# A pair's second projection in the eight-tile form, and the LayerNorm steps laid out anew, in a two-layer graph attention kernel

## What is computed

```python
# 4 heads of 64; the 2048 columns of the scores fall into 8 segments of 256
q, k, v = x @ Wq.T + bq, x @ Wk.T + bk, x @ Wv.T + bv
scores = einsum(q, k) / sqrt(64)           # per head and segment
scores = clip(scores, -10, 10); scores = where(adj == 0, -10, scores)
ctx = sum over the segments of softmax(scores in the segment) @ v
out = layernorm(ctx @ Wo.T + bo + x) * gamma + beta     # "first LayerNorm"
x1 = layernorm(x + out)                                  # "second LayerNorm"
```

## Time and profile before

| | us |
|---|---|
| three runs | 4062.63 to 4076.89, median 4069.85 |
| the profiled execution's own time | 4073.17 |
| its span, first to last instruction | 4071.4 |
| mean granted clock of TensorE | 0.972 of full speed |
| busy: TensorE, VectorE, ScalarE, GpSimd | 3657.9, 3294.2, 2519.2, 2045.2 |

### The profile page before, as it was taken

One profiled execution on the slowest core, in us unless ns is written; L12 is line 12 of the kernel. 1 busy time (PEld: TensorE's weight loads), 2 busy tenths in 40 slices (PEclk: granted clock), 3 DMA queues, 4 the chain that ended last, 5 costly groups with the idle time before them and its releaser, 6 DMA issues. The chain is left out here.

```text
span 4071.4 us, 131728 instructions
## 1 busy us (share of the span) xinstructions
PE 3657.9 (90%) x55412; PEld 2507.9 (62%) x55412; DVE 3294.2 (81%) x3989; ACT 2519.2 (62%) x3554; POOL 2045.2 (50%) x1068
## 2 busy tenths in 40 slices
PE   5999999999999999999999999952998999899988
PEld 2656656655665665666565566421777777777777
DVE  6786787787688678678778768858889889899897
ACT  3665665566566566566566566631776776676777
POOL 1776776777677677677667767742011011011010
PEclk9999999999999999999999999976999999999999
DMA  5000010001000000001000100024110110101101
GB/s 211 3 34 13 13 45 13 13 14 44 13 14 34 13 24 34 13 13 45 13 13 14 44 13 13 13 68 175 32 52 21 53 51 23 53 27 46 32 21 42
DMA packets 106678, 145.05 MB, mean 36 GB/s; under 512 B 3792, under 2 KB 87632, under 8 KB 104016
## 3 DMA queue, kind: packets, MB, share of 16 engines
q1 hardware_dynamic: 104816, 135.80, 10.0%
q10 hardware_dynamic: 1248, 0.40, 0.1%
HBM read 102.63 MB, written 33.55 MB: 33 GB/s over the span
## 5 line engine op out<-in xcount | busy, mean ns | idle before, releaser
L373 ACT ACTIVATE probs<-probs 128x1024 f32<-128x1024 f32 x1024 | 1083.9, 1059 | 997.2 <-DVE probs L778 971.5
L269 POOL TENSOR_TENSOR psums<-probs 128x1024 f32<-128x1024 f32 x512 | 1265.6, 2473 | 788.4 <-ACT probs L373 757.1
L778 DVE SCALAR_TENSOR_TENSOR probs<-sc_ps,clip_hi 128x1024 f32<-128x1024 f32 x1024 | 1228.5, 1216 | 442.9 <-PE sc_ps L472 436.5
L485 PE MATMUL ctx_ps<-probs,v_rows 64*32 64x512 f32 x16256 | 1385.1, 593 | 0.0
L472 PE MATMUL sc_ps<-q_cols,k_cols 64*32 64x512 f32 x16384 | 1209.2, 593 | 96.9 <-DVE probs L778 88.5
L1242 PE MATMUL out_ps<-wh,e 128*128 128x257 f32 x4096 | 963.1, 388 | 168.4 <-DVE e L1384 162.3
L1242 PEld LDWEIGHTS out_ps<-wh,e 128*128 128x128 f32 x4096 | 777.1, 193 | 329.7 <-DVE e L1384 125.6
L485 PEld LDWEIGHTS ctx_ps<-probs,v_rows 64*32 64x32 f32 x16256 | 659.2, 107 | 250.2 <-issue 143.8
L472 PEld LDWEIGHTS sc_ps<-q_cols,k_cols 64*32 64x32 f32 x16384 | 548.1, 107 | 413.4 <-issue 293.6
L479 PE MATMUL den_ps<-psums,ones 64*32 64x512 f32 x4064 | 610.5, 599 | 54.2 <-ACTq L324 18.9
L1071 POOL TENSOR_TENSOR rstd<-var_eps,minus_half 128x4 f32<-128x4 f32 x32 | 68.4, 2138 | 1071.1 <-DVE var_eps L1344 1071.1
(11 more groups left out here) (97 smaller groups left out, 3325.6 us busy)
## 6 DMA issues: line engine op xcount, KB each, us to landing
x_cols<-in_xT SPq DMA_DIRECT2D x8, 2048.0 KB, 10.4
probs<-in_adjT SPq DMA_DIRECT2D x16, 1024.0 KB, 8.3
x_rows<-in_x SPq DMA_DIRECT2D x32, 512.0 KB, 4.9
x<-res SPq DMA_DIRECT2D x32, 512.0 KB, 3.3
x_in<-x SPq DMA_DIRECT2D x8, 2048.0 KB, 10.3
x_res<-x SPq DMA_DIRECT2D x32, 512.0 KB, 4.6
out<-h SPq DMA_DIRECT2D x32, 512.0 KB, 3.2
e<-in_adjT SPq DMA_DIRECT2D x8, 1024.0 KB, 7.8
```

Source lines behind the costliest of these rows:

```text
L269: pool.tensor_tensor(psums[:, q % 2, pair, :], probs[:, (SJ * q) % RING, pair, :], probs[:, (SJ * q + 1) % RING, pair, :], ALU.add).then_i ...
L373: act.activation(probs[:, n % RING, pair, :], probs[:, n % RING, pair, :], ACT.Exp, scale=DH ** -0.5).then_inc(s_exp, 1)
L485: return pe.matmul(ctx_ps[quad(h), z, :], v_rows[head_rows(r), n % JB, at:at + QUAD], probs[head_rows(r), n % RING, h, :], start=start, st ...
L778: dve.scalar_tensor_tensor(out=probs[:, n % RING, pair, :], in0=sc_ps[:, p, :, :], scalar=-LIM, in1=clip_hi[:, j, c * CW:(c + 1) * CW][:, ...
```

## The change

A pair with two projections gets its own order, `pair_with_two`: the second projection in the eight tiles too, its lower half beside the context part between the third and fourth scores, its upper half behind the fourth scores together with the rest of the contexts. ScalarE copies a second projection ahead of the exponential (n+1,1), not behind it. The projections are spread anew over the steps: seconds stand at the steps 1, 3, 9, 57, 59, 61 and 63 (before: 1, 5, 11, 53, 57, 59, 61), seven as before, and pairs 9 and 10 gain a first while pairs 13 and 14 lose theirs. VectorE's LayerNorm steps go to other slots: of `times_gamma`, `add_x`, `add_bo` and `add_beta` no pair has more than two, where pair k = 7 had three. `inverse_deviation` and `norm` follow by one pair, and the SyncE queue takes the load of x_cols, the load of x rows and the store of x1 in another order.

```diff
@@ -57,17 +57,18 @@
-    uses = {0: ("k", 3, 0), 1: ("v", 2), 2: ("k", 3, 1), 4: ("v", 3), 5: ("q", 1, 0), 10: ("v", 4), 11: ("q", 1, 1),
-            12: ("v", 5), 14: ("v", 6), 16: ("v", 7), 26: ("q", 2, 0), 28: ("q", 2, 1), 32: ("q", 3, 0),
+    uses = {0: ("v", 2), 1: ("k", 3, 0), 2: ("k", 3, 1), 3: ("q", 1, 0), 4: ("v", 3), 9: ("q", 1, 1), 10: ("v", 4),
+            12: ("v", 5), 14: ("v", 6), 16: ("v", 7), 18: ("q", 2, 0), 20: ("q", 2, 1), 32: ("q", 3, 0),
             34: ("q", 3, 1)}
...
-    NEXT = {48: ("q", 0, 0), 50: ("q", 0, 1), 52: ("k", 0, 0), 53: ("k", 0, 1), 57: ("k", 1, 0), 58: ("k", 1, 1),
-            59: ("v", 0), 60: ("k", 2, 0), 61: ("v", 1), 62: ("k", 2, 1)}
+    NEXT = {48: ("q", 0, 0), 50: ("q", 0, 1), 52: ("k", 0, 0), 57: ("k", 0, 1), 58: ("k", 1, 0), 59: ("v", 0),
+            60: ("k", 1, 1), 61: ("v", 1), 62: ("k", 2, 0), 63: ("k", 2, 1)}
     assert not set(uses) & set(NEXT)
...
     PRJ = len(order)
+    SECOND = [n for n in order if n % 2]
     FIRST = len(NEXT)
@@ -87,6 +88,10 @@
         return count(b, PRJ, FIRST + order.index(n) - skipped)
+
+    def second_number(b, n, more):
+        skipped = 0 if more else sum(other < n for other in NEXT if other % 2)
+        return count(b, len(SECOND), SECOND.index(n) - skipped)
@@ -170,6 +175,8 @@
         s_waited = sem("waits_over")
+        s_stored = sem("stores_begun")
+        s_part2 = sem("first_rows_of_second_projection_added")
         s_pool = sem("segment_summed")
@@ -218,17 +225,18 @@
                 sp.wait_ge(s_n[1], count(b, NC * T, (c + 1) * T))
+                sp.sem_inc(s_stored, 1)
                 sp.dma_start(batch_of(x1, b)[c * CW:(c + 1) * CW, :].rearrange("(t p) f -> p t f", p=P),
...
             def chunk(b, c, prev, more):
-                if prev == 2:
-                    store_x1(*back(b, c - 2, NC))
-                load_rows(b, c)
                 if c == 2 and more:
...
                                  .rearrange("(k p) n -> p k n", p=P)).then_inc(s_xT, 16)
+                load_rows(b, c)
+                if prev == 2:
+                    store_x1(*back(b, c - 2, NC))
@@ -291,7 +299,7 @@
                         inverse_deviation(*back(b, c - 1, NC), 0)
-                    if k == 2 and prev == 2:
+                    if k == 3 and prev == 2:
                         inverse_deviation(*back(b, c - 2, NC), 1)
@@ -380,22 +388,22 @@
                     if prev and k in (6, 7):
-                        norm(*back(b, c - 1, NC), 1 + 2 * (k - 6), 0)
-                    if prev == 2 and k in (3, 4):
-                        norm(*back(b, c - 2, NC), 2 * (k - 3), 1)
+                        norm(*back(b, c - 1, NC), 2 * (k - 6), 0)
+                    if prev == 2 and k in (4, 5):
+                        norm(*back(b, c - 2, NC), 2 * (k - 4), 1)
                     exponential(b, n, 1)
...
                     exponential(b, n + 1, 0)
-                    if prev and k in (5, 6):
-                        norm(*back(b, c - 1, NC), 2 * (k - 5), 0)
-                    if prev == 2 and k in (3, 4):
-                        norm(*back(b, c - 2, NC), 2 * (k - 3) + 1, 1)
-                    exponential(b, n + 1, 1)
+                    if prev and k in (6, 7):
+                        norm(*back(b, c - 1, NC), 2 * (k - 6) + 1, 0)
+                    if prev == 2 and k in (4, 5):
+                        norm(*back(b, c - 2, NC), 2 * (k - 4) + 1, 1)
                     if second:
                         take(*second, use_number(b, n + 1, more))
+                    exponential(b, n + 1, 1)
@@ -604,6 +612,72 @@
+            def pair_with_two(b, n, at, q, of, use, number, of2, use2, number2, nth):
+                scores(b, n, 0)
+                sums_ready(at, q)
+                pe.wait_ge(s_prjfree, number + 1)
+                waited()
+                for h in range(HEADS):
+                    den_part(q, 0, h)
+                    prj_part(of, use, 1, 0, h, 0, start=True)
+                for h in range(HEADS):
+                    prj_part(of, use, 1, 0, h, 1)
+                contexts_ready(at, q)
+                for h in range(HEADS):
+                    ctx_part(q, 0, 0, 0, h, start=True)
+                    prj_part(of, use, 1, 1, h, 0)
+                for h in range(HEADS):
+                    last = prj_part(of, use, 1, 1, h, 1)
+                last.then_inc(s_part, 1)
+                scores(b, n, 1)
+                other_rows_done(at, q, 0)
+                for h in range(HEADS):
+                    prj_part(of, use, 0, 0, h, 0)
+                    last = den_part(q, 1, h)
+                for h in range(HEADS):
+                    prj_part(of, use, 0, 0, h, 1)
+                last.then_inc(s_den, 1)
+                for h in range(HEADS):
+                    prj_part(of, use, 0, 1, h, 0)
+                    ctx_part(q, 1, 1, 0, h, start=True)
+                for h in range(HEADS):
+                    last = prj_part(of, use, 0, 1, h, 1, stop=True)
+                last.then_inc(s_prj, 1)
+                for h in range(HEADS):
+                    ctx_part(q, 0, 0, 1, h)
+                    last = ctx_part(q, 1, 1, 1, h)
+                last.then_inc(s_part, 1)
+                scores(b, n + 1, 0)
+                other_rows_done(at, q, 1)
+                pe.wait_ge(s_prjfree, number2 + 1)
+                waited()
+                for h in range(HEADS):
+                    ctx_part(q, 0, 1, 0, h)
+                    prj_part(of2, use2, 1, 0, h, 0, start=True)
+                for h in range(HEADS):
+                    prj_part(of2, use2, 1, 0, h, 1)
+                for h in range(HEADS):
+                    ctx_part(q, 0, 1, 1, h, stop=True)
+                    prj_part(of2, use2, 1, 1, h, 0)
+                for h in range(HEADS):
+                    last = prj_part(of2, use2, 1, 1, h, 1)
+                last.then_inc(s_part2, 1)
+                scores(b, n + 1, 1)
+                pe.wait_ge(s_part2, nth + 1)
+                waited()
+                for h in range(HEADS):
+                    prj_part(of2, use2, 0, 0, h, 0)
+                    ctx_part(q, 1, 0, 0, h)
+                for h in range(HEADS):
+                    prj_part(of2, use2, 0, 0, h, 1)
+                for h in range(HEADS):
+                    prj_part(of2, use2, 0, 1, h, 0)
+                    last = ctx_part(q, 1, 0, 1, h, stop=True)
+                last.then_inc(s_pv, 1)
+                for h in range(HEADS):
+                    last = prj_part(of2, use2, 0, 1, h, 1, stop=True)
+                last.then_inc(s_prj, 1)
+
             def context(b, q):
@@ -655,11 +729,16 @@
                                 project(*first, use_number(b, n, more))
+                    elif first and second:
+                        pair_with_two(b, n, at, q, *first, use_number(b, n, more),
+                                      *second, use_number(b, n + 1, more), second_number(b, n + 1, more))
+                        continue
                     elif first:
...
                     if second:
+                        pe.sem_inc(s_part2, 1)
                         project(*second, use_number(b, n + 1, more))
@@ -786,24 +865,26 @@
                     if prev == 2 and k == 0:
+                        times_gamma(*back(b, c - 2, NC), 1)
+                    if prev == 2 and k == 1:
+                        add_x(*back(b, c - 2, NC), 1)
+                    if prev == 2 and k == 2:
+                        stats(*back(b, c - 2, NC), 2)
+                        stats(*back(b, c - 2, NC), 3)
+                    if prev and k == 3:
+                        add_bo(*before, 1)
+                    if prev and k == 5:
+                        variance(*before, 0)
+                    clip(b, n, 1)
+                    if prev == 2 and k == 0:
+                        add_x(*back(b, c - 2, NC), 0)
+                    if prev == 2 and k == 1:
                         stats(*back(b, c - 2, NC), 0)
                         stats(*back(b, c - 2, NC), 1)
-                    if prev and k == 1:
+                    if prev and k == 2:
                         add_bo(*before, 0)
-                    if prev and k == 2:
-                        add_beta(*before, 0)
-                    if prev and k == 7:
-                        add_x(*before, 0)
-                    clip(b, n, 1)
-                    if prev == 2 and k == 0:
-                        stats(*back(b, c - 2, NC), 2)
-                        stats(*back(b, c - 2, NC), 3)
-                    if prev and k == 1:
-                        add_bo(*before, 1)
-                    if prev == 2 and k == 1:
+                    if prev == 2 and k == 2:
                         variance(*back(b, c - 2, NC), 1)
-                    if prev and k == 2:
-                        add_beta(*before, 1)
                     used = use_at(b, n, more)
@@ -812,12 +893,10 @@
                             dve.sem_inc(s_prjfree, TO)
-                    if prev and k == 4:
```

(10 more changed lines are left out.)

## The result

The changed kernel took 3979.97 us (median of 4, 3976.71 to 3980.59) against 4072.03 us (median of 4, 4062.63 to 4076.89): a ratio of 0.9775, interval 0.9756 to 0.9794, 92 us less. Forecast were 144 us less, range 3885 to 3995. The sign and the range held; the gain was two thirds of the forecast, because LayerNorm steps and the loop cost what the forecast hadn't priced. A later run of the same file gave 3981.39.

A forecast was written before the change was run, and what follows sets the result against it. TensorE was taken to bound layer 0, late by 30 us a batch. Terms -3.6 - 5.1 + 1.0 - 9.7 - 2.0 = -19.4 us a batch, -144 in total, gave 3926 us; range 3885 to 3995.

The forecast's parts named there:

- What bounds: Layer 0: TensorE sets the time; only its lateness of 30 us a batch can be won; layer 1 isn't touched.
- Tiling: Second projections in eight tiles instead of four: the 0.51 us for two tiling changes goes, seven times, -3.6 us a batch.
- Copy ahead of the exponential: Pairs with a second projection: denominators late by 0.39 or 0.30 us, 2.55 where 7.7 was, -5.1 us a batch.
- New waits in mid-pair: Seconds need `prj_ps` free earlier, before the fourth scores: +1.0 us a batch for seven pairs, both ends 0.3 and 5.
- Late `normalise`: Pairs with a second: `normalise` starts about 2.5 us later, the last clip behind it; cost nothing, up to 0.5 each.
- LayerNorm steps: VectorE's steps in new slots of layer 0: clips late by 4.5 where 14.2 was, -9.7 us a batch.
- The cheap side: Single slot B steps in seven pairs without projection, asked about 0.2 us before GpSimd changes operation: 0.5 each, 3.5 us.
- The rest: Denominators waiting for GpSimd's sums at pairs 11 and 18 no longer late: 1.2 of 3.2 stays, -2.0 us a batch.
- the first rival: New waits eat half, at pairs 0 and 1, pairs without projection and late `normalise`: -64 us, 4006; chance 0.11.
- The second: Rival: only the projections gain, since steps find GpSimd busy wherever they go: -58 us, 4012; chance 0.07.
- the third: Rival: slower, fourth clip behind late `normalise` delays the next pair's first copy, 4.2 us a second: +70, 4140; chance 0.05.
- the fourth: Rival: no change, the won time comes back as waits for GpSimd's sums: 4070; chance 0.03.

## Why the forecast was right, and where a term was mis-sized

- *What bounds.* Right: TensorE's work didn't change, layer 1 neither, and the whole gain is lateness between starts.
- *Tiling.* Forecast -3.6, measured -3.4 us a batch. The trace agrees with the draining that the Trainium skill states (TensorEngine Tiling (Array Packing), Key Properties): 0.51 us for two changes of tiling before, 0.02 us at the same place after. The same page's warning that different row tiles can't use one PSUM bank at the same time (Restrictions and Gotchas, PSUM Pressure) isn't tried by any run here, since a wait keeps the two halves apart; the scores behind a second's upper half start within 0.03 us of their nominal time.
- *Copy ahead of the exponential.* Forecast -5.1, measured -3.8: the chain took 0.56 + 0.69 + 0.19 us in the pair, not the start-up's 0.08 + 0.69 + 0.09 behind a matmul that ends at 0.39.
- *New waits in mid-pair.* Forecast 1.0, measured 1.3, up to 0.64 in pair 1. *Late `normalise`*: forecast nothing, and nothing by itself; copying behind it would have cost 224 us, some 65 of them by the clock.
- *LayerNorm steps.* This is the term that failed in size: 4.5 forecast, 8.2 measured, with 3.6 for the turn on top. Four things were wrong in it. (1) I asked of slot A only whether the clips and scores still fit; behind the clip (n,1) stand four operations of ScalarE that end in `normalise`, and I didn't follow them: 4.8 us, for a step (`add_x` at k = 1) that the sum has at nothing. (2) "The cheap side" at pairs without projection: pairs 13 and 21 fell on the dear one, 1.4 each, by 0.07 us, because `variance` had left k = 4 and GpSimd started earlier; pairs 14, 15, 22 and 23 cost little (0.3 at most). The bound of 1.6 held, the choice of 0.5 a pair didn't; that the seven together cost no more than the 3.5 I took is luck. (3) Under the 3 us of pair 15 lay the turn of the loop. A wait that ends last hides the one beneath it; pair 23, equal but for the turn, was late by 2.9 us against 3.1, so nothing in the rows of before priced it. (4) I took the clock for full. The 14.2 us of late clips before hold 1.3 at pair 24 that were TensorE at half clock behind the wait of pair 23, and after it is 1.1 of the turn's 3.6.
- *The rest.* Forecast -2.0; the waits for sums at pair 11 went, pair 18 got another cause.
- *Rivals.* The result lies 26 us from the first rival (4006) and 54 from the forecast; its mechanism, GpSimd's whole operations, is half of the deficit, though at other pairs than 0 and 1. The second is refuted by the slots' 46 us, the third and the fourth by the result. The third had its place right: with the copy behind the exponential its chain is there.

## What to carry to other kernels

Before counting a removed wait as gain, ask what else happens at that place, a loop's jump above all, and compare places with and without it; the kernel before can't show it while the longer wait covers it. Where two engines lock each other for whole operations, a step costs 0.7 or 2.9 us by a tenth of a microsecond: put such a step where the dear case is free (here slot B of a pair with a projection), not where it is likely to be cheap. Follow a delayed instruction through every queue behind it, not only to the next user of its result. And look at the granted clock behind TensorE's longest waits: here such a wait often cost another 1.7 us that no releaser in the rows explains.

## What the runs showed of the hardware that I had not expected

A jump back of the loop over batches, with bodies of thousands of matmuls, cost TensorE 2.5 us of "issue" before its next scores and 3.0 us a batch in all; with a body twice as long 5.4 us. The same instructions in a loop and written out differ by 4 us a batch even where no jump falls. Which of two engines gets in first was settled by under 0.1 us, in the changed kernel the same way in all six inner batches; in the written-out loop the `add_x` of pair 9 took 0.68 us in six batches and 2.94 in the seventh, with starts 0.02 us apart. And in a kernel in which TensorE is 90% busy the granted clock still fell to half for a moment behind many of its longest waits: in the eight batches of layer 0 never in the written-out changed kernel, 4 times in the changed one, 11 times before, 42 times with the copy behind the exponential.
